# Expert mixture on one NeuronCore: tokens as the stationary operand, expert weights streamed in pairs as high and low parts, routing weights applied after the product

## What is computed

```python
rw = _gating(hidden_states, sim_matrix, gates)      # (b, t, 16), softmax over the chosen experts
q = einsum('bte,bted->btd', rw, einsum('btc,ecd->bted', hidden_states, q_proj))   # e = 16, c = 128, d = 64
k = einsum('bte,bted->btd', rw, einsum('btc,ecd->bted', hidden_states, k_proj))
v = einsum('bte,bted->btd', rw, einsum('btc,ecd->bted', hidden_states, v_proj))
attn = softmax(causal(q @ k.T / 8)) @ v
mixed = attn[:, :, None, :] * rw[..., None]
out = einsum('bted,edc->btc', mixed, o_proj)
```

## Time and profile before

| | |
|---|---|
| runs | 271.34, 273.94, 274.54 us, median 273.94 |
| the profiled execution | 271.15 us, its span (first to last instruction) 269.4 us |
| busy share of the span | PE 85%, DVE 70%, ACT 41%, POOL 31% |
| mean granted TensorE clock | 0.949 of 2.4 GHz |

### The profile page before, as it was taken

The page is one execution under the profiler, slowest core; times in us unless marked ns, Lnnn a source line. Parts: engine busy times, 40 slices in busy tenths (PEclk is TensorE's granted clock), DMA queues, the critical chain, the costliest instruction groups (busy, mean ns, idle before and its releaser), DMA issues.

```text
span 269.4 us, 5466 instructions
## 1 busy us (share of the span) xinstructions
PE 227.7 (85%) x2015; PEld 192.2 (71%) x2020; DVE 188.8 (70%) x528; ACT 111.2 (41%) x250; POOL 84.8 (31%) x115
## 2 busy tenths in 40 slices
PE   0627383899999999999789999997799769999995
PEld 0516382799999999998678877886576547777773
DVE  2799987768844855755957398865989799446553
ACT  1314363022212213213224276674795936544443
POOL 2365340140000101101100031131687566555551
PEclk9999959799999999999875899999799999999999
DMA  4993000000000000000000000000000000010001
GB/s 123 420 393 96 2 0 0 0 2 1 2 0 4 0 0 2 1 2 0 4 0 2 0 2 2 5 2 0 2 0 0 4 0 0 1 39 2 0 0 39
DMA packets 4169, 7.78 MB, mean 29 GB/s; under 512 B 592, under 2 KB 2608, under 8 KB 4016
## 3 DMA queue, kind: packets, MB, share of 16 engines
q1 hardware_dynamic: 3952, 7.38, 7.5%
q10 hardware_dynamic: 192, 0.07, 0.1%
HBM read 6.92 MB, written 0.52 MB: 28 GB/s over the span
## 4 chain that ended last, share of the span: by engine, by line
PE 60%; DVE 27%; ACT 4%; issue 3%; DMA 3%; POOL 1%; SPq 1%; DVEq 0%; ACTq 0%
PE psum L1246 15%; PE psum L1431 9%; PE psum L1297 6%; PE psum L1474 5%; PE psum L1372 3%; PE psum L1332 3%; PE psum L1228 3%; DMA xr<-x_dram 3%; DVE negm L959 2%; PE psum L1359 2%; DVE st L697 2%; DVE kw L784 1%; PE psum L1355 1%; PE psum L1318 1%; DVE hm L1017 1%
## 5 line engine op out<-in xcount | busy, mean ns | idle before, releaser
L357 POOL TENSOR_TENSOR rstd<-ve,m 128x1 f32<-128x1 f32 (+1 forms) x20 | 12.9, 643 | 117.9 <-DVE ve L702 117.9
L1246 PE MATMUL psum<-wqkv,hm 128*128 128x192 f32 x256 | 49.6, 338 | 0.0
L1246 PEld LDWEIGHTS psum<-wqkv,hm 128*128 128x128 f32 x256 | 42.0, 194 | 0.0
L425 POOL TENSOR_TENSOR qs<-hm,qs 128x512 fp32r<-128x512 f32 (+1 forms) x26 | 33.8, 1300 | 22.4 <-ACT qs L614 22.4
L910 DVE TENSOR_TENSOR hm<-xn2T,psum 128x512 f32<-128x512 f32 x32 | 21.8, 684 | 20.0 <-PE psum L1228 19.8
L1431 PE MATMUL psum<-x4hi,ks 128*128 128x512 f32 (+1 forms) x56 | 23.4, 418 | 3.5 <-issue 3.1
L959 DVE TENSOR_REDUCE negm<-psum 128x8 f32<-128x1024 f32 x16 | 19.5, 1221 | 9.6 <-PE psum L1332 9.6
L1474 PE MATMUL psum<-qs,wdhi 128*128 128x512 f32 (+1 forms) x56 | 25.8, 470 | 0.1
L629 ACT ACTIVATE hm<-psum 128x512 f32<-128x512 f32 (+1 forms) x28 | 16.7, 597 | 21.9 <-PE psum L1456 13.1
L1017 DVE TENSOR_TENSOR hm<-hm,psum 128x512 f32<-128x512 f32 x22 | 15.1, 687 | 13.3 <-ACT hm L629 13.2
L570 ACT ACTIVATE exT<-psum 128x1024 f32<-128x1024 f32 x16 | 16.4, 1023 | 17.7 <-PE psum L1359 17.7
(11 more groups left out here) (211 smaller groups left out, 504.7 us busy)
## 6 DMA issues: line engine op xcount, KB each, us to landing
wqkv<-wqkv_dram SPq DMA_DIRECT2D x1, 1536.0 KB, 10.7
wa<-wa_dram SPq DMA_DIRECT2D x1, 880.0 KB, 12.4
wb<-wb_dram SPq DMA_DIRECT2D x1, 880.0 KB, 12.8
...
wo<-wo_dram SPq DMA_DIRECT2D x1, 512.0 KB, 11.2
```

What stands on the lines that cost most here:

```text
L425: return nc.gpsimd.tensor_tensor(dst, src, hi.bitcast(F32), ALU.subtract)
L1246: last = mm(bank[:, 0:3 * HD], hm[:, b % 2, e, :], wqkv[:, e, :], start=(e == 0), stop=(e == E0 - 1))
```

## The change

The product is turned round. The stationary operand is now the tokens `x` themselves (channels x tokens), and two experts' weights (384 columns) stream past in one matmul. The routing weight is then a number per output partition (token) and per expert, applied to the product. To keep the precision without f32 matmuls, tokens and weights are split in a high and a low part (type fp32r), and three matmuls are added up per pair of experts: xhi·whi, xhi·wlo, xlo·whi.

- `high_qkv` (ACT, 4 instructions of 128x768) and `low_qkv` (POOL, 8 of 128x384) split the weights; `low_qkv(0)` to `(3)` stand ahead of `rstd_of(3, ...)` on POOL, `low_qkv(4)` behind it, 5 to 7 behind `low_keys(1)`. `take_xn2T` writes `xhi` too (ACT), `low_x2` the low part (POOL).
- `project(j)` (PE): two pairs of experts per step, three matmuls of 128x384 each; four PSUM banks in turn. The even pair goes to ACT, the odd one to DVE.
- `scale_experts(j)` (ACT): two activations of 128x192 with the routing weight as scale. `add_parts` (POOL, three per sequence, 128x384) and `add_both` (POOL, 128x192) add them up.
- `sum_experts(j)` (DVE): two instructions of 128x192, product times weight plus the running sum.
- `join_experts(b)` (DVE, at s = 4b+4): adds DVE's two halves, waits for POOL's `both`, and writes `qk` and `v2`.
- Gone: `spread`, `scale_hidden`, `take_qkv`, `sel` with its 128x2048 activation. `rw` is kept for all sequences. `gate_exp(0)` stands behind two more `take_ks` on ACT.

```diff
-        hm = sb("hm", [C, 2, E0, T])
+        whi = sb("whi", [C, E0, 3 * HD], F32R)
+        wlo = over("wlo", [C, E0, 3 * HD], F32R, "wqkv")
+        xhi = sb("xhi", [C, NB, T], F32R)
+        xlo = sb("xlo", [C, NB, T], F32R)
+        sumd = sb("sumd", [T, 2, 2, 3 * HD])
+        suma = sb("suma", [T, 2, 2, 3 * HD])
+        part = sb("part", [T, 2, 2, 3 * HD])
+        both = sb("both", [T, 2, 3 * HD])
...
+        def expert_bank(c):
+            return (4, 6, 0, 2)[c % 4]
...
+            def low_qkv(c):
+                e = slice(2 * c, 2 * c + 2)
+                pool.wait_ge(qkvhi_ready, c // 2 + 1)
+                nc.gpsimd.tensor_tensor(wlo[:, e, :], wqkv[:, e, :], whi[:, e, :].bitcast(F32), ALU.subtract).then_inc(qkvlo_ready, 1)
...
+            def low_x2(hf):
+                pool.wait_ge(xn2T_ready, hf + 1)
+                pool.wait_ge(xhi_ready, hf + 1)
+                nc.gpsimd.tensor_tensor(xlo[:, bs(hf), :], xn2T[:, bs(hf), :], xhi[:, bs(hf), :].bitcast(F32), ALU.subtract).then_inc(xlo_ready, 1)
...
             power(sim2[:, :], sim2[:, :], simr_ready)
-            for hf in range(2):
-                rstd_of(3 + hf, 1, HALF * hf, HALF * hf + HALF)
-                pool.wait_ge(hn_ready, hf + 1)
-                power(rhn[:, bs(hf)], hn[:, bs(hf)], rhn_ready)
-                if hf == 0:
-                    low_keys(1)
+            for c in range(4):
+                low_qkv(c)
+            rstd_of(3, 1, 0, HALF)
+            low_qkv(4)
+            pool.wait_ge(hn_ready, 1)
+            power(rhn[:, bs(0)], hn[:, bs(0)], rhn_ready)
+            low_x2(0)
+            low_keys(1)
+            for c in range(5, E0 // 2):
+                low_qkv(c)
+            rstd_of(4, 1, HALF, NB)
+            pool.wait_ge(hn_ready, 2)
+            power(rhn[:, bs(1)], hn[:, bs(1)], rhn_ready)
+            low_x2(1)
...
+            def add_parts(b, i):
+                pool.wait_ge(act_took, 4 * b + i + 2)
+                if i:
+                    pool.wait_ge(suma_ready, 3 * b + i)
+                nc.gpsimd.tensor_tensor(suma[:, b % 2, :, :], suma[:, b % 2, :, :], part[:, i % 2, :, :], ALU.add).then_inc(suma_ready, 1)
+            def add_both(b):
+                pool.wait_ge(suma_ready, 3 * b + 3)
+                if b >= 2:
+                    pool.wait_ge(qk_ready, b - 1)
+                nc.gpsimd.tensor_tensor(both[:, b % 2, :], suma[:, b % 2, 0, :], suma[:, b % 2, 1, :], ALU.add).then_inc(both_ready, 1)
...
-            for b in range(NB):
-                rstd_of(5 + b, 2, b, b + 1)
-                add_bc(b)
-                if b in (2, 4):
-                    fill_vm(b // 2 - 1)
+            for s in range(4 * NB + 20):
+                for b in range(NB):
+                    if 4 * b + 1 <= s < 4 * b + 4:
+                        add_parts(b, s - 4 * b - 1)
+                    if s == 4 * b + 3:
+                        add_both(b)
+                    if s == 4 * b + 15:
+                        rstd_of(5 + b, 2, b, b + 1)
+                        add_bc(b)
+                        if b in (2, 4):
+                            fill_vm(b // 2 - 1)
...
+                nc.scalar.activation(xhi[:, bs(hf), :].rearrange("p b t -> p (b t)"), PB[6 + hf][:, :], ACT.Copy).then_inc(xhi_ready, 1)
...
+            def high_qkv(c):
+                e = slice(4 * c, 4 * c + 4)
+                nc.scalar.activation(whi[:, e, :], wqkv[:, e, :], ACT.Copy).then_inc(qkvhi_ready, 1)
+            act.wait_ge(ld_qkv, 16)
+            high_qkv(0)
+            high_qkv(1)
             high_keys(0)
-            nc.scalar.activation(sel[:, :, :], bc(part16[:, :], 2, 128), ACT.Copy).then_inc(c_sel, 1)
+            high_qkv(2)
+            high_qkv(3)
             exp_channels(1)
...
-            def take_qkv(b):
...
+            def scale_experts(j):
+                b, c = j // 4, 2 * (j % 4)
+                act.wait_ge(rw_ready, b // HALF + 1)
+                act.wait_ge(experts_ready, 8 * b + c + 1)
+                bank = PB[expert_bank(c)]
+                if c == 0:
+                    into = suma[:, b % 2, :, :]
+                    if b >= 2:
+                        act.wait_ge(both_ready, b - 1)
+                else:
+                    i = c // 2 - 1
+                    into = part[:, i % 2, :, :]
+                    if b >= 1 or i == 2:
+                        act.wait_ge(suma_ready, (3 * b, 3 * b - 1, 3 * b + 1)[i])
+                for i in range(2):
+                    ins = nc.scalar.activation(into[:, i, :], bank[:, 3 * HD * i:3 * HD * i + 3 * HD], ACT.Copy,
+                                               scale=rw[:, b, 2 * c + i:2 * c + i + 1])
+                ins.then_inc(act_took, 1)
...
-            def scale_hidden(i):
...
+            def sum_experts(j):
+                b, c = j // 4, 2 * (j % 4) + 1
+                dve.wait_ge(experts_ready, 8 * b + c + 1)
+                bank = PB[expert_bank(c)]
+                if j % 4:
+                    dve.wait_ge(dve_took, j)
+                elif b >= 2:
+                    dve.wait_ge(qk_ready, b - 1)
+                for i in range(2):
+                    w = rw[:, b, 2 * c + i:2 * c + i + 1]
+                    x = bank[:, 3 * HD * i:3 * HD * i + 3 * HD]
+                    if j % 4:
+                        ins = V.scalar_tensor_tensor(out=sumd[:, b % 2, i, :], in0=x, scalar=w, in1=sumd[:, b % 2, i, :], op0=ALU.mult, op1=ALU.add)
+                    else:
+                        ins = V.tensor_scalar(sumd[:, b % 2, i, :], x, w, None, ALU.mult)
+                ins.then_inc(dve_took, 1)
+            def join_experts(b):
+                total = sumd[:, b % 2, 0, :]
+                dve.wait_ge(dve_took, 4 * b + 4)
+                link(V.tensor_tensor(total, total, sumd[:, b % 2, 1, :], ALU.add))
+                dve.wait_ge(both_ready, b + 1)
+                if b >= 2:
+                    dve.wait_ge(aT_ps, b - 1)
+                V.tensor_tensor(qk[:, b % 2, :], total[:, 0:2 * HD], both[:, b % 2, 0:2 * HD], ALU.add)
+                V.tensor_tensor(v2[:, b % 2, :, :], bc(total[:, 2 * HD:3 * HD], 1, 2), bc(both[:, b % 2, 2 * HD:3 * HD], 1, 2), ALU.add).then_inc(qk_ready, 1)
...
+            def project(j):
+                b = j // 4
+                if j % 4 == 0:
+                    pe.wait_ge(xlo_ready, b // HALF + 1)
+                for c in (2 * (j % 4), 2 * (j % 4) + 1):
+                    bank = PB[expert_bank(c)]
+                    if b == 0:
+                        pe.wait_ge(qkvlo_ready, c + 1)
+                        if c == 0:
+                            pe.wait_ge(x1_ready, 1)
+                        if c == 2:
+                            pe.wait_ge(ks_ready, 7)
+                    if 8 * b + c >= 4:
+                        pe.wait_ge(dve_took if c % 2 else act_took, 4 * b + c // 2 - 1)
+                    e = slice(2 * c, 2 * c + 2)
+                    for n, (x, w) in enumerate(((xhi, whi), (xhi, wlo), (xlo, whi))):
+                        last = mm(bank[:, 0:6 * HD], x[:, b, :], w[:, e, :].rearrange("p e d -> p (e d)"), start=(n == 0), stop=(n == 2))
+                    last.then_inc(experts_ready, 1)
+            project(0)
             for b in range(HALF, NB):
                 turn_keys(b)
+            project(1)
             pe.wait_ge(c_sel, 1)
...
-            def spread(i):
...
-            def project(i):
...
+                if 2 <= s + 1 < 4 * NB:
+                    project(s + 1)
```

95 lines of the change are left out of this document (28 added, 67 removed).

## The result

| | before | changed |
|---|---|---|
| runs taken together | 271.34 to 276.43, median 274.24 us | 287.20, 287.45, 291.01, 295.04, median **289.23 us** |
| ratio, 95% interval | | **1.056 [1.040, 1.072]**: slower |
| profiled execution, its span | 271.15, 269.4 | 295.04, 293.2 |
| busy share PE, DVE, ACT, POOL | 85, 70, 41, 31% | 79, 70, 44, 42% |
| granted clock, whole span | 0.949 | 0.878 |

The account below looks back on a forecast made before the run. PE was taken to bound the loop, its saving to go into DVE's work and waits: 1.6 + 3.4 + 5.9 + 0 + 1.4 = 12.3 us on 271.15 gives 283.5, plus 1.5 for the median: 285 us, range 271 to 297.

Parts of the forecast that it names:

- forecast case: Whole kernel: PE's saving goes into DVE's added work and waits, 285 us (279 to 291); chance 0.55 together with rival 4.
- rival 1: TensorE's granted clock falls within the loop, 8 us more, 293 us; chance 0.15.
- The start: Up to `after_channels(1)`: POOL's weight splits delay logits and gating, less work falls away; +1.6 us.
- The first join: `join_experts(0)` waits for POOL's late clearing and sums, so `turn_qk(0)` comes at 64.7; +3.4 us beyond the start.
- Steps 5 to 13: From `turn_qk(0)` to the first `project_o`: DVE alone takes 21.6 us for 15.7; +5.9 us (+3 to +8).
- the gating's stops: Steps 5 to 13: five gate steps on DVE each meet an `add_parts` on POOL; 3.5 us (1 to 5).
- the eight pairs: Steps 5 to 13: DVE's eight pairs of scaled products take 4.6 us.
- The steady periods: Distance between `project_o` in the loop: no change, 10.5 us (9.9 to 11.2); the last period +1.4 us.
- PE's part: PE per loop period: 7.0 us go, 4.3 come, 7.8 us left, so PE no longer bounds.
- Rival 3: PE's saving reaches the end because the join's and `project_o` waits vanish, periods 8.6, 262 us; chance 0.1.
- Rival 4: The new matmuls take 0.232 us each, PE 9.1 per period; forecast plus 1 us; chance within the forecast's 0.55.
- The lock on the pairs: DVE's new pairs read PSUM and aren't locked by POOL; if they were, about 10 us more.

Follow-up runs that it names:

- e6: Changed kernel with join and `turn_qk`/`take_qkT` late, POOL's clearing early, two weight splits and `low_qkv(4)` behind the root for `rhn`: 279.27 us, ratio 1.019.
- e3: Changed kernel with POOL's three sums per sequence on 8 of 192 columns, the rest left out of the result: 276.49 us, ratio 1.022.
- e4: Changed kernel with sixteen unread matmuls of 128 columns ahead of `turn_qk`'s wait, to hold the clock: 290.03 us, ratio 1.068.
- e9: Changed kernel with join and `turn_qk` late and POOL's sums on 8 of 192 columns, the rest left out: 268.66 us, ratio 0.986.
- e1: Changed kernel with POOL's clearing of `wparts`, `msp` and `vm` moved ahead of `rstd_of(4)`: 289.85 us, ratio 1.073.

## Why the prediction was right

Forecast 285 (271 to 297), slower with 0.7; measured 289.23. The forecast case came, with a part of rival 1.

- **The start, right.** `after_channels(1)` was forecast at +1.6 and came at +1.0 (50.12 for 49.08). The gating, 11.1 us by the forecast, took 11.2 (38.36 to 49.56). What was less is the delay of the logits, 38.36 for 39.0: POOL's long root began at 24.74 and not at 25.71 as in the earlier trace rows, so all that queues behind it came earlier.
- **The first join, right.** `turn_qk(0)` forecast 64.7, came at 65.23, behind an idle DVE (5.71 us) that `both` releases. e6 shows that this is a price: when the queue is opened, 3.9 us come back ahead of the first `project_o`.
- **Steps 5 to 13, right as a sum, in part by luck.** 21.6 forecast, 20.9 measured (65.23 to 86.16). The terms were off in both directions: the gating's stops came to 1.9 (0.47, 0.63, 0.69 and 0.08) and not 3.5, the eight pairs took 5.3 and not 4.6, and the two joins with their waiting 4.2 (72.72 to 74.75 and 82.78 to 84.94) and not 3.5. e3 takes 3.8 us off this stretch (63.82 to 80.95 is 17.1), which looks like the 3.5 of stops and is not: 1.9 are the stops, 1.5 the waits at the two joins, the rest lies between the first join and `turn_qk(0)`.
- **The steady periods, mis-sized.** "No change, 10.5 us" is 10.9 to 11.3 at full clock (e4). The waits were nearly right, by the timeline of e4 at full clock:

```profile
99.32 0.29 DVE L1045 TENSOR_TENSOR xr<-xr,psum 128x128 f32<-128x128 f32 x1 [0.65 <-PE psum L1383]
...
102.73 0.69 DVE L1040 TENSOR_TENSOR mixT<-aT,psum 128x512 f32<-128x512 f32 x1 [0.35 <-PE psum L1374]
...
103.97 0.35 DVE L781 TENSOR_SCALAR xna<-xr,mv,rstd 128x128 f32<-128x128 f32 x1 [0.56 <-POOL rstd L370]
...
105.01 1.03 DVE L1001 TENSOR_TENSOR sumd<-sumd 128x192 f32<-128x192 f32 x1
106.58 0.29 DVE L1005 TENSOR_TENSOR qk<-sumd,both 128x128 f32<-128x128 f32 x1 [0.54 <-POOL both L460]
```

  At the join DVE stands 0.54 for `both` and 0.67 locked on the first sum (1.03 for 0.36), together 1.2 where I had 1.5; for `project_o` 0.65, where I had 1.0; for `normalise`'s root 0.56, where I had 0.5. DVE's own work was short: 10.88 less these and the 0.35 ahead of the mix leaves 8.1, where I had 7.35. A pair of products takes 0.66 from start to start (66.67 to 67.33 in the changed kernel) and not 0.57, which is 0.3 in four; the other 0.4 I can't place row by row. Over five periods I had +1.4, and e4 has +4.8: 2.4 in the first four, which I had at nothing, and 2.4 in the fifth.
- **PE's part, wrong by 0.8, without effect on the time.** "PE per period would be 7.8 us": e9 shows 8.59. I had taken the spreads by their busy time, 1.56 per sequence; by the distance of starts four take 0.9. And the first of the new matmuls behind other work comes 0.09 later than the rest, 24 of them take about 4.6 for my 4.3. Rival 3's 262 us asked for periods of 8.6 with every wait gone; e9 removes nearly all of them and reads 268.7.
- **Rival 1, the clock, in part.** It does fall behind the join's hole, but not at every join. Its price was put at 8 us on the sum; runs of the changed kernel at a mean clock of 0.910 and at 0.872 to 0.878 differ by about that, 287.2 and 295 us, and its median lies between. In the loop alone it was 7 us in the longest run and 1.6 in that of e1. With more holes in PE the mean clock was lower: 0.949 before, 0.878 changed, 0.849 with a third of the matmuls away. The Trainium skill ("TensorE: Matmul & The Clock Gate", The HAM clock gate) says that half rate is the default and activity releases it; for the means the trace agrees. I had given this rival 0.15, and wrote that by this rule it would be likelier.
- **Rival 4, excluded.** The new matmuls start 0.173 us apart at full clock, not 0.232.
- **The lock on the pairs, excluded.** They read PSUM and take 0.41 beside POOL's sums or not. I had missed that `join_experts` itself adds two SBUF operands (its first sum, 1.04 to 1.21 for 0.36 at five of eight joins), though in the changed kernel this mostly hides in the wait for `both` behind it. The Trainium skill ("SBUF — State Buffer", Who interferes with whom) also names `tensor_scalar`, copies and casts as able to enter the two-port modes that lock; the trace agrees: `pn`, a `tensor_scalar` within SBUF, took 0.83 for 0.29 in e6, and the cast at 79.71 took 0.89 for 0.20. There these stops are on the path.

What stays open: why the clock falls behind some holes and not behind others of the same length, and so how much of the 1.6 to 7 us at low clock could be had. e4 held the clock in the loop of its profiled run, its other three runs were not profiled, and its median shows no gain.
